# The first gate of a two-layer graph and experts kernel: ranks behind the down matmuls, and one block with the first experts stage

## The reference, cut to what matters

```
x = x + L0_gnn(layernorm(x))      # 128 x 64 tokens of 128 numbers
x = x + L0_ffn(layernorm(x))      # 8 experts, the two best of each token
x = x + L1_gnn(layernorm(x))
x = x + L1_ffn(layernorm(x))      # 8 experts, the best of each token

# L0_gnn: _, U = eigh(normalized Laplacian)
h = relu(einsum('mn,bnd->bmd', U.T, f) @ W1 + b1)
out = einsum('nm,bmd->bnd', U, h @ W2 + b2)
# L0_ffn: w, i = top_k(x @ Wg + bg, 2), w = softmax(w)
out = sum over e of w_e * (gelu(x @ W1[e] + b1[e]) @ W2[e] + b2[e])
```

## Time and profile before

| what | value |
|---|---|
| runs | 1497.54 us (1496.87 to 1500.97) |
| profiled execution | 1496.8 us, span 1494.9 us |
| busy: PE, DVE, ACT, POOL | 1135.6, 829.1, 761.8, 556.3 us |
| first gate, first mixing matmul | at 335.89 us |
| first experts stage, first transpose | at 492.43 us |

### The profile page before, as it was taken

The page is one execution under the profiler, slowest core; times in us unless marked ns, Lnnn a source line. Parts: engine busy times, 40 slices in busy tenths (PEclk is TensorE's granted clock), DMA queues, the critical chain, the costliest instruction groups (busy, mean ns, idle before and its releaser), DMA issues. The chain is left out here.

```text
span 1494.9 us, 28100 instructions
## 1 busy us (share of the span) xinstructions
PE 1135.6 (76%) x6361; PEld 831.8 (56%) x6362; DVE 829.1 (55%) x3890; ACT 761.8 (51%) x2089; POOL 556.3 (37%) x855
## 2 busy tenths in 40 slices
PE   2444422729662799999977998999999879929995
PEld 1233312617551699999974554445544335519995
DVE  4777799977664333345447773444444468722221
ACT  3555544604330466666645775566555456515552
POOL 3666614700456774045537610000000005654554
PEclk9999965659865899999987999999999989969998
DMA  9400000000011233233322100000000001233330
GB/s 261 125 1 1 1 1 0 2 0 5 29 40 61 90 119 102 70 101 103 103 67 52 43 11 0 1 0 0 0 0 0 4 1 68 83 131 109 106 104 26
DMA packets 85702, 75.59 MB, mean 51 GB/s; under 512 B 13206, under 2 KB 74847, under 8 KB 85612
## 3 DMA queue, kind: packets, MB, share of 16 engines
q1 hardware_dynamic: 71788, 44.64, 10.8%
q0 software_dynamic: 13824, 29.98, 6.3%
HBM read 41.72 MB, written 33.37 MB: 50 GB/s over the span
## 5 line engine op out<-in xcount | busy, mean ns | idle before, releaser
L1211 POOL DMA_INDIRECT z<-spent,seats x64 | 62.8, 981 | 401.8 <-DVE spent L1332 381.8
L1677 ACT ACTIVATE c_H<-ps,c_b 128x128 f32<-128x128 f32 x576 | 156.9, 383 | 98.4 <-PE ps L1722 98.4
L2186 PE MATMUL ps<-BIG,spent 128*128 x364 | 156.1, 578 | 3.3 <-ACTq L2199 3.3
L1722 PE MATMUL ps<-c_ZT,c_w 128*128 128x128 f32 x1152 | 143.6, 279 | 4.1 <-ACT c_ZT L1666 2.8
L1708 PE MATMUL ps<-spent,c_H 128*128 x1152 | 140.3, 275 | 0.0
L1722 PEld LDWEIGHTS ps<-c_ZT,c_w 128*128 128x128 f32 x1152 | 137.1, 195 | 5.1 <-ACT c_ZT L1666 3.5
L1708 PEld LDWEIGHTS ps<-spent,c_H 128*128 128x128 f32 x1152 | 134.3, 192 | 0.0
L2186 PEld LDWEIGHTS ps<-BIG,spent 128*128 128x128 f32 x364 | 69.7, 192 | 84.6 <-issue 84.6
L2194 PE MATMUL ps<-e_hs,spent 128*128 128x512 f32 (+1 forms) x256 | 110.0, 572 | 0.0
L861 POOL DMA_INDIRECT z<-BIG,spots x64 | 63.0, 984 | 119.7 <-DVE spots L980 102.0
L1551 POOL DMA_INDIRECT c_rows<-y,seats x64 | 60.5, 946 | 115.4 <-DMA y<-c_ys 60.8
(11 more groups left out here) (507 smaller groups left out, 2673.9 us busy)
## 6 DMA issues: line engine op xcount, KB each, us to landing
BIG<-z SPq DMA_DIRECT2D x72, 129.0 KB, 2.0
c_Z<-z SPq DMA_DIRECT2D x144, 64.0 KB
y<-c_ys SPq DMA_DIRECT2D x72, 128.0 KB
spent<-in_L_ffn_W_dram SPq DMA_DIRECT2D x1, 2048.0 KB
spent<-in_L_ffn_W_dram SPq DMA_DIRECT2D x8, 256.0 KB
w_dn<-in_L_ffn_Wd_dram SPq DMA_DIRECT2D x8, 256.0 KB
z<-BIG,spots POOLq DMA_INDIRECT x128, 2.2
z<-j_padding SPq DMA_DIRECT2D x9, 129.0 KB, 2.6
```

What stands on the lines that cost most here:

```text
L1211: pool.indirect_dma_start(z, bass.IndirectOffsetOnAxis(ap=k.seats[:, 0, n:n + 1], axis=0), k.R[:, row(n), :], None, bounds_check=E * STRID ...
L1677: act.activation(H[u][:, c, h * P:(h + 1) * P], UP[u][c // 2][:, o:o + P], ACT.Gelu, bias=b1[u][h][:, c:c + 1]).then_inc(gelu, 1)
L1722: pe.matmul(UP[u][c // 2][:, o:o + P], w1[u][h][:, c * P:(c + 1) * P], ZT[u][:, h * P:(h + 1) * P], start=True, stop=True).then_inc(up, 1)
L2186: last = pe.matmul(view(k.ps[4 * u + j], wide, lanes), k.w_ihT[:, w, :], state(i, u, s, p, wide, lanes), start=True, stop=(s == 0))
```

## The change: order inside the gate, and one block

In the gate, four things change. VectorE's `add_bias` of an even group stands ahead of the multiply of the ranks. The gate's bias add moves from the end of a step to the start of the next, which is the same place in VectorE's row. TensorE's `rank` stands behind the down matmuls of its step. The multiply of the ranks releases a semaphore of its own, `rank_read`, and the gate matmuls wait for this and no longer for `seated`.

`gnn0_gate0` and `experts_in` become functions that return one part for each engine, and `gate0_experts_in` runs them in one block. GpSimd and TensorE then wait for `tabled`, which VectorE releases at the end of its tables, SyncE waits for `tabled`, the zero rows and all scatters of the first choice. GpSimd itself no longer waits for its scatters. The tiles `Z` and `ZT` of the experts stage lie in `ZB` and `ZS`, which exist anyway.

```
             def seat(q):
                 dve.wait_ge(ranked, q + 1)
-                got = link.put(tt_(prod[:, :, :, :], RANK.rearrange(...), k.chosen[:, tiles_of(q), :, :], ALU.mult))
+            tt_(prod[:, :, :, :], RANK.rearrange(...), k.chosen[:, tiles_of(q), :, :], ALU.mult).then_inc(rank_read, 1)
                 yield
-                link.need(got)
+            dve.wait_ge(rank_read, q + 1)
...
             for g in range(GROUPS + LAG + 3):
+            if LAG + 2 <= g <= GROUPS + LAG + 1:
+                add_gate_bias(g - LAG - 2)
                 if g % 2 == 0 and 0 <= q_seat < PAIRS:
                     beside = seat(q_seat)
-                    next(beside)
...
                 if g < GROUPS:
                     add_bias(g)
+            if g % 2 == 0 and 0 <= q_seat < PAIRS:
+                next(beside)
...
-                if LAG < g <= GROUPS + LAG:
-                    add_gate_bias(g - LAG - 1)
...
-                if ranks:
-                    rank((g - 11) // 2)
                 if 1 <= g <= GROUPS:
...
                     last.then_inc(dn_done, 1)
+            if ranks:
+                rank((g - 11) // 2)
...
                     if ranks:
-                        pe.wait_ge(seated, (g - 11) // 2 + 1)
+                    pe.wait_ge(rank_read, (g - 11) // 2 + 1)
...
-            pool.wait_ge(scattered, 16 * TILES)
...
+        dve.sem_inc(tabled, 1)
...
-        Z = [mine(f"Z{u}_", [P, P], HALVES) for u in range(2)]
-        ZT, ys, H = mine("ZT", [P, SLOT_TILE]), mine("ys", [P, HALVES, D]), mine("H", [P, C, SLOT_TILE])
+    Z = [[k.ZB[u][:, h * P:(h + 1) * P] for h in range(HALVES)] for u in range(2)]
+    ZT = [buf[:, 0:SLOT_TILE] for buf in k.ZS]
...
+    def experts_sync(sp):
+        sp.wait_ge(k.gate0_tabled, 1)
+        sp.wait_ge(k.gate0_padded, 16 * (E + 2))
+        sp.wait_ge(k.gate0_scattered, 16 * TILES)
...
-        gnn0_gate0(nc, k, sem, z0)
-        experts_in(nc, k, sem, z0, y0)
+        gate0_experts_in(nc, k, sem, z0, y0)
```

More of the change, by code:

```diff
@@ L822, in gnn0_gate0 @@
     RANK, COUNT = GA[:, GC // 2:GC // 2 + PAIR * PICKS * E], TR[:, 0:PICKS * E]
[L823 to L862, removed]
-            pool.wait_ge(scattered, 16 * TILES)
[L865 to L898, removed]
-                got_both = link.put(tt_(both[:, :], ve, vo, ALU.add))
-                link.put(tt_(total[:, :], me, mo, ALU.add))
-                next(other, None)
-                link.need(got_even)
-                link.put(tt_(var[:, :], var[:, :], var[:, :], ALU.mult))
-                link.need(got_both)
-                got = link.put(ts_(both[:, :], both[:, :], 1.0 / D, EPS, ALU.mult, ALU.add))
@@ new lines, in mine @@
+    def mine(name, shape, dtype=F32):
+        return own.enter_context(nc.sbuf_tensor("a_" + name, shape, dtype))
+    O, HT = ([mine(f"{n}{u}", [P, GC]) for u in range(2)] for n in ("O", "H"))
+    var, both, total, bits, half, root = (mine(n, [P, PAIR]) for n in ("var", "both", "total", "bits", "half", "root"))
+    m1, m2, ex = (mine(n, [P, TILES]) for n in ("m1", "m2", "ex"))
+    tied, first, prod = mine("tied", [P, PAIR, E]), mine("first", [P, PAIR]), mine("prod", [P, PAIR, PICKS, E])
+    sums, part = mine("sums", [P, PAIRS + 1, PICKS * E], BF16), mine("part", [P, PICKS * E])
@@ new lines, in finish @@
+        def finish(work):
+            for _ in work:
+                pass
+        dve.tensor_copy(k.ones16[:, :], k.ones[:, :])
+        dve.tensor_copy(k.upper16[:, :], k.upper[:, :])
+        link.put(dve.memset(sums[:, 0, :], 0.0))
+        link(dve.memset(k.zero[:, :], 0.0))
+        dve.sem_inc(s_zero, 1)
+        for c in range(PICKS):
+            got = link.put(ts_(stretch[:, c, :], k.irow[:, 0:E], float(STRIDE), float(c * WING), ALU.mult, ALU.add))
+        link.need(got)
+        link(ts_(whole[:, :, :], stretch[:, :, :], 1.0 / P, None, ALU.mult))
@@ new lines, in gate_vector @@
+        link(ts_(blocks[:, :], blocks[:, :], P.bit_length() - 1, None, ALU.logical_shift_right))
+        link(dve.tensor_copy(nb[:, :, :].rearrange(by_pick), blocks[:, :]))
+        link.put(ts_(gap[:, :, :], nb[:, :, :], -float(P), float(STRIDE), ALU.mult, ALU.add))
+        link.put(dve.tensor_copy(k.pads[:, :], padat[:, 1, :]))
+        for c in range(PICKS):
+            got = link.put(dve.tensor_tensor_scan(end[:, c, :], k.ones[:, 0:E], nb[:, c, :], float(c * REGION), ALU.mult, ALU.add))
@@ L1649, in _ @@
[L1649 to L1660 removed]
+            gate[2](dve)
+            experts[2](dve)
         @block.scalar
@@ L1681, in _ @@
[L1681 to L1686 removed]
+            gate[3](act)
+            experts[3](act)
         @block.tensor
         def _(pe):
[L1690 to L1699 removed]
@@ L1729, in one @@
-            def one(t):
-                step(t, t % 2, t // 2, t + 1)
-            turn(0, 0, 0, 0)
-            for t in range(4):
-                one(t)
-            paired(pe, step, 4, SECOND - 2)
-            for t in range(SECOND - 2, SECOND):
-                one(t)
-            paired(pe, step, SECOND, NT - 2)
-            for t in range(NT - 2, NT + 1):
-                one(t)
+            gate[4](pe)
+            experts[4](pe)
 def rounds(eng, step, tiles, first, last):
```

836 lines of the change are left out of this document (452 added, 384 removed).

## The result

The changed kernel took 1483.24 us, the median of 4 runs (1480.51 to 1489.99), beside 1499.26 us for the kernel before in 4 runs (1496.87 to 1504.29): ratio 0.9891, 95% interval 0.9848 to 0.9933, so faster, by 1.1%. The forecast was 1480 in a range of 1475 to 1487. The profiled execution took 1481.0 us (span 1478.8), 15.8 under the one of before (1496.8, span 1494.9) where the sum of the prediction had said 17.3; by the medians of four runs each the gain is 16.0. A later comparison of the same kernel gave 0.9899 (0.9876 to 0.9922) in five runs from 1480.63 to 1487.68; one more execution was slow (4274 us at a mean clock of 0.298) and is left out.

What follows compares the result with a forecast made beforehand. The prediction took the first gate's three first periods, then GpSimd's gapless scatters, as the bound. From 1496.8 us profiled, -11.5 (order) and -5.8 (block) gave 1479.5, plus 0.7 to the median: 1480 us, range 1475 to 1487.

Steps and rivals of the forecast that it cites:

- (a): First gate, first pair: bias add ahead of the ranks' multiply brings the seats and GpSimd's first scatter 2.1 us earlier.
- (b): First gate: three periods between ranks shrink from 50.18 us to 35.7 to 40.2, starting pair 3's scatters 11.5 us earlier.
- the mixed clock of the pair above: TensorE's chain from gate matmuls to down matmuls takes 5.86 us partly at low clock, giving 13.8 us a period.
- the middle, 38.0: First gate: sum of three periods taken between 35.7 us (full clock) and 40.2 us (mixed clock).
- the near bound: First gate: smallest gain allowed for the start of pair 3's scatters, 9.3 us; the largest was 13.8.
- (c): Gate to experts: one block cuts last scatter to TensorE's first transpose from 12.05 us to 6.2, saving 5.8 us.
- (d): Everything else, including tables, moved expert tiles and VectorE's earlier weight copies, was costed at nothing.
- 1 (clock full): First gate: clock stays full, three periods total 35.7 us, time 1478 us; chance 0.20.
- 2: Block edge saves little because GpSimd's 5.3 us drain may be work paid later; time 1486 us; chance 0.06.
- 3: First gate: TensorE's chain at low clock takes back half the gain, three periods 44.0 us, 1486 us; chance 0.09.
- Rival 4: First gate: TensorE stays at 1.2 GHz from the first ranks and becomes the bound, 1502 us; chance 0.03.
- VectorE's wait: Sign in the first gate: VectorE's waits for TensorE's down matmuls fall from 21.4 us to under 8.

Runs made afterwards that it cites:

- block_only: The changed kernel with the old order inside the gate, keeping the one block for two stages: 1495.48 us, ratio 0.9961 to the kernel before.
- the repeat: The changed kernel itself measured again with nothing changed, on the same chip as three others: 1485.86 us, ratio 0.9899 to the kernel before.
- order_only: The kernel before with the new order inside the gate, keeping its two blocks: 1489.26 us, ratio 0.9921 to the kernel before.
- warm_start: The changed kernel plus 44 unused matmuls in TensorE's idle before the experts' first transpose: 1487.97 us, ratio 0.992 to the kernel before.
- warm_long: The changed kernel plus 57 unused matmuls in TensorE's idle before the experts' first transpose: 1484.6 us, ratio 0.9905 to the kernel before.
- filled: The changed kernel plus unused matmuls on TensorE right ahead of ranks 0 to 3: 1479.51 us, ratio 0.9857 to the kernel before.

## Why the prediction was right, and where it was off

(a) First seats: forecast 2.1 us earlier. VectorE's multiply stands at R + 1.11 with R the start of the ranks, and the seats are 1.6 us earlier; ranks 0 themselves were 0.6 later (377.67 for 377.07), as the whole gate was by 0.4 at its first mixing matmul (336.25 for 335.89). The mechanism is right.

(b) The step that was mis-sized is TensorE's chain between the gate's matmuls and `a_O`, and with it the sum of three periods. Its terms, held against the first period: gate's matmuls at R + 1.56, measured 1.55; from `a_O` to the next ranks 6.42, measured 6.43. Between them stands TensorE's chain, for which the prediction took 4.16 us at the full clock or 5.86 in "the mixed clock of the pair above", so `a_O` at R + 5.7 or R + 7.4. It came at R + 8.28: the chain took 6.7 us because the clock was low from 378 to 384. Before, the clock was low at the ranks and the down matmuls, was back while TensorE waited for the seats, and fell again only in the middle of the chain, whose gate matmuls from 381.92 had still run at full speed (1.03 us). After 0.50 at 378 to 380, the next stretches of two us of the kernel before, columns as above:

```profile
380.00:382.00 2.00, 0.08 (x1) 0.12 (x2) 1.96 (x8) 0.00 (x0) 0.00 (x0) 0.92 0.00 0
382.00:384.00 2.00, 2.00 (x18) 2.00 (x19) 1.76 (x12) 0.53 (x1) 1.26 (x1) 0.93 0.00 0
384.00:386.00 2.00, 2.00 (x6) 1.24 (x6) 0.31 (x3) 1.26 (x4) 1.40 (x2) 0.50 0.20 70
```

So the 5.86 us that the prediction called mixed were measured in a chain whose beginning ran at the full clock. That the wait for the seats gave the clock back is not shown: block_only has the same wait, and its clock stayed at 0.50 through it. Now the chain starts 1.55 us behind the ranks, and its first four parts lie in the low stretch. The upper bound of 13.8 us a period was no bound: the first period passed it by 0.9, the second was under it (13.44), the third at the 12.6 given. And "I take the middle, 38.0" supposed that half of the periods would see the full clock; both of the first two had a low stretch in the chain, and the third as well, and so it was in all five executions with this order. Sum 40.7 for 38.0 (the bound was 40.2), 42.3 in the repeat, 40.4 to 41.8 in order_only, warm_start and warm_long: none came near the middle. Pair 3 came 8.65 us sooner for the 11.5 forecast, under the 9.3 of the near bound.

The sentence that TensorE's idle "falls from 5.1 us to about 2.2" was near, 2.72 in the first period (2.25 and 0.47), but less idle did not keep the clock up. The Trainium skill (TensorE: Matmul & The Clock Gate, "HAM oscillation - how this bites in real kernels"), which the prediction read as speaking for 13.8 us a period, is borne out in kind: a low stretch came in each period, behind waits of 2.25 to 2.55 us, which are shorter than those of the page's example. In filled it came behind 0.71 and 0.48 us.

(c) The edge of the block: forecast 6.2 us for 12.05, measured 6.21. The load 3.39 us behind the last scatter as in the earlier trace rows was 3.61. Right, and for the reason given.

(d) The rest at nothing: nothing in the experts stage grew by what the gate gained. Its 1.7 us less is inside the spread of the table (283.5 to 286.6), so it is put down to nothing.

The sum came nearer than its terms. What was forecast up to the first transpose was 17.3 us, and 14.6 came (8.8 and 5.8); the 1.7 us of the experts stage, which no term had, bring the profiled pair to 16.1. That is luck. By the medians the forecast of 1480 was 3.2 us too low: 1.5 in the sum, and the rest in the step from the profiled execution to the median, 2.2 us for the 0.7 taken from three runs.

The rivals: 1 (clock full) is refuted by the 0.50 in each of the first two periods, though filled shows its price for a full period to be about right (11.74 us for 12.1; all three took 37.7 for 35.7, as only one was full); 2 by block_only; 3 asked for 44.0 us of periods and 1486 us, and the truth, 40.7 and 42.3 in the repeat, lies between it and the forecast: its mechanism, TensorE's chain at the low clock taking part of the gain back, is the one that acted, at 0.4 to 0.7 of the size. Rival 4 had the same mechanism in its extreme. Of what the prediction said would show it, two things did not come: ranks 1 were 14.71 us behind ranks 0 (12 to 14), and VectorE's wait was 14.9 us (under 8). The repeat's first period, 15.01, even just passed the 15 that the prediction called wrong.

## What to carry to other kernels

Where one engine's chain is bound by another engine's chain, count how much of that chain will stand under the low clock once its waits are moved: here a wait of 1.07 us cost 1.8 to 3.5. The same code had the clock at other places in other executions (50.2 and 53.2 us for three periods of the old order, 40.4 to 42.3 of the new), so a chain's price at "the clock as it was" is worth no more than the one execution it was read in. In a step order written by hand, work that a waiting engine needs goes ahead of work that nobody waits for, but only from the group on at which somebody does wait. A block edge behind indirect DMAs can be priced from another edge of the same program. Warming TensorE up bought nothing here, since its next wait was for another engine.

## What the runs showed that was not expected

- The clock fell to 0.50 in filled at 392 us with TensorE busy in all but 0.7 us of the gap before the ranks; it was low for some 3.4 us there, and for some 6.8 us in the first period of the changed kernel.
- With the same order and the same wait of 1.95 us for the seats the clock was back at full speed in the kernel before (0.92 from 380 to 382) and not in block_only (0.50).
- TensorE's first turns of the experts stage at 1.00 or at 0.50 leave the stage's length as it is (284.1 and 283.5 us).
- The stretch behind `d_Y`, the same code in all kernels, took 717.2 to 722.1 us: a profile a kernel can't tell 5 us there.
